# Sorting tokens by expert for two batches at a time, and sharing the copies of the transposed probabilities between two engines

## The chip, the core and the metric

The kernel runs on one core of a Trainium2 chip. The metric is the device time of one execution in microseconds (us). A core has five engines that run side by side, each through its own queue of instructions in order: TensorE (PE), VectorE (DVE), ScalarE (ACT), GpSimd (POOL) and SyncE (SP, which here only starts transfers). They wait for each other through semaphores.

## What is computed

```python
x = L0_attn_x                                   # (16, 512, 256), float32
xn = _layernorm(x, axis=-1)
x = x + attn(xn, wqkv, wo, q_norm_w, k_norm_w) + ffn(xn, gate_w, expert_w)

def attn(x, ...):                               # 16 heads of 64
    q, k, v = split(einsum('btc,oc->bto', x, wqkv))
    q = _rope(_rmsnorm(q, q_norm_w), cos, sin)  # k alike
    attn = softmax(causal(einsum('bhtd,bhsd->bhts', q, k) * 64 ** -0.5))
    return einsum('btc,oc->bto', einsum('bhts,bhsd->bhtd', attn, v), wo)

def ffn(x, gate_w, expert_w):                   # 8 experts of 256 x 256
    onehot = one_hot(argmax(einsum('bsh,eh->bse', x, gate_w), -1), 8)
    expert_out = einsum('bsh,efh->bsef', x, expert_w)
    return x + einsum('bsef,bse->bsf', expert_out, onehot)
```

Each token uses one of eight experts, the one with the highest gate score. The choice is known only while the kernel runs.

## The kernel before

The work is cut into 128 units: 16 batches of 512 tokens times 8 pairs of heads. A batch has NT = 4 row tiles of 128 tokens. Float32 products are made of three products of rounded halves (TERMS), over two chunks of the 256 inputs (NC = 2), so a 128-token tile times one weight block is six matmuls.

Each engine's program is written out by hand as a function unit(u), called for u = -1 to 130. In unit u, PE does the attention of unit u, the q, k and v products of unit u+1, and the values (L494) of unit u-1. All engines follow one pattern of four score blocks k = 0 to 3, of 256, 512, 384 and 128 columns per head (ITEMS, L28):

- scores(u, k) on PE (L466) writes ps_s, which exists once, so it waits for the exponentials of the block before.
- row_max(u, k) on DVE (L631) reads ps_s, softmax(u, k) on ACT (L342) writes prob.
- transpose_probs(u, k) on PE (L483) writes ps_p, which exists once too, and take_pt(u, k) on ACT (L350) copies both heads of it to prob_t.

Between the blocks, PE makes q, k and v of the next unit in four tiles (qkv, L431); ACT squares and copies them (take_qkv, L324); DVE multiplies by the rotation tables (rope_products, L612); POOL rotates and scales (L278, L286). At the end of the unit PE transposes the result (transpose_qk, L458), ACT takes the rounded halves k_t and q_t and DVE the remainders (take_qk, L337 and L625). Only then can scores(u+1, 0) start. The output of unit u-1 is normalised by DVE (normalise_o, L642) with the reciprocals that PE transposed (L506) and ACT copied (take_inverse, L356), is split by ACT and DVE (take_o, L363 and L647), and project(u) on PE (L449) adds it through take_projection (L662).

The experts are dense: in each unit PE multiplies all four row tiles of the batch by one expert, the one with the pair's number (experts, L440), 24 matmuls in two halves, one before the fourth score block and one after transpose_qk. DVE multiplies each result by the token's onehot column and adds it to acc (take_experts, L652). Some pairs of a batch carry more on DVE: pair 0 choose (L599), pair 4 row_stats (L569), pair 5 normalise_x (L580), pair 6 the transposed xn of the next batch (take_xt, L587), pair 7 start_rows (L593). Three PSUM banks ps_g0 to ps_g2 serve all other products in turn; g_bank (L189) works out whose turn it is, and bank (L409) waits until the use three turns back has been read:

```python
            def bank(i, *released):
                for sem, n in until[i]:
                    pe.wait_ge(sem, n)
                until[i] = released
                return ps_g[i]
```

Before the first unit the weights are loaded in seven chunks, four of w_qkv, two of w_exp and one of w_out, and DVE splits each into halves (L722 to L726).

## Time and profile before

| | us |
|---|---|
| median of three runs (lowest, highest) | 2467.36 (2464.22, 2468.24) |
| the profiled execution, its own time | 2465.25 |
| its span, first to last instruction | 2463.1 |
| busy in the span: PE / DVE / ACT / POOL | 2352.5 / 1755.1 / 1450.9 / 1172.1 |

The granted clock of PE is 0.997 of full speed as a mean over the span. A group of instructions (in the list by line) gives the busy time and the mean time of one; instructions overlap a little, so the start-to-start distance in the timeline is shorter than the duration. In the timeline a bracket at the end of a row says how long the engine was idle before it and what released it. "PEld" is PE's weight load, which runs beside its matmuls.

### The profile page before, as it was taken

To read this page: it belongs to the slowest core of one execution; us is meant where nothing else is said; L and a number is where in the kernel's file an instruction comes from. 1 tells how busy PE (TensorE), PEld (TensorE's weight loads), DVE (VectorE), ACT (ScalarE), POOL (GpSimd) and SP (SyncE) were. 2 spreads that over 40 slices of the span, in tenths; PEclk is the share of its full clock that TensorE was granted. 3 is DMA by queue.
4 is the path that set the end of the run, shared out by engine and by line. 5 is a ranking of instruction groups with operands and counts; after the bars stand their busy time and mean duration, and the time that the engine had idled before them with its cause. 6 is when DMAs were issued, how large, how long until landed. Compare 5 with 4: busy or idle time off the path is not lost.

```text
span 2463.1 us, 49058 instructions
## 1 busy us (share of the span) xinstructions
PE 2352.5 (96%) x18048; PEld 1947.8 (79%) x18048; DVE 1755.1 (71%) x4009; ACT 1450.9 (59%) x4193; POOL 1172.1 (48%) x1822
## 2 busy tenths in 40 slices
PE   2999999999999999999999999999999999999998
PEld 1788788878888887887888888788878878888886
DVE  5677777777767777777777777767777776777775
ACT  1656566655665656665665666566556656655664
POOL 1554544455454445545544444554445445445442
PEclk9999999999999999999999999999999999999999
DMA  3000000000000000000000000000000000000000
GB/s 125 1 1 6 14 1 18 1 6 14 1 18 1 18 1 1 18 1 18 1 6 14 1 18 1 5 14 1 18 1 12 8 1 18 1 18 1 5 6 9
DMA packets 19596, 26.53 MB, mean 11 GB/s; under 512 B 1952, under 2 KB 18464, under 8 KB 18976
## 3 DMA queue, kind: packets, MB, share of 16 engines
q1 hardware_dynamic: 19360, 23.41, 3.0%
q8 instruction: 145, 2.38, 0.4%
q14 instruction: 91, 0.75, 0.1%
HBM read 15.02 MB, written 8.39 MB: 10 GB/s over the span
## 4 chain that ended last, share of the span: by engine, by line
PE 73%; DVE 16%; ACT 8%; issue 2%; DMA 1%; POOL 0%; SPq 0%; DVEq 0%
PE ps_g L419 34%; PE ps_s L476 13%; PE ps_o L502 12%; PE ps_p L491 8%; ACT prob L346 4%; PE ps_s L479 4%; DVE k_t L628 3%; DVE q_t L628 3%; DVE neg_max L634 3%; ACT k_t L340 2%; PE ps_g L510 2%; DVE o_n L645 1%; DVE ln_stat L573 1%; DVE xn L583 1%; DVE onehot L609 1%
## 5 line engine op out<-in xcount | busy, mean ns | idle before, releaser
L283 POOL TENSOR_TENSOR qk_rot<-qk_cos,qk_sin 128x128 f32<-128x128 f32 x1024 | 445.5, 456 | 1203.1 <-DVE qk_sin L620 1196.5
L346 ACT ACTIVATE prob<-ps_s,neg_max 128x256 f32<-128x256 f32 (+3 forms) x1024 | 530.8, 523 | 618.6 <-DVE neg_max L634 603.7
L419 PE MATMUL ps_g<-w_qkv,xn_t 128*128 128x384 f32 (+1 forms) x3072 | 604.3, 346 | 28.6 <-DVE xn_t L590 28.6
L419 PEld LDWEIGHTS ps_g<-w_qkv,xn_t 128*128 128x128 f32 x3072 | 529.2, 189 | 29.0 <-issue 29.0
L634 DVE TENSOR_REDUCE neg_max<-ps_s 128x2 f32<-128x512 f32 (+3 forms) x512 | 419.3, 819 | 119.9 <-PE ps_s L479 119.9
L620 DVE TENSOR_TENSOR qk_cos<-ps_g,t_cos 128x256 f32<-128x256 f32 x512 | 214.9, 420 | 352.6 <-ACT v L335 352.3
L353 ACT ACTIVATE prob_t<-ps_p 128x512 f32<-128x512 f32 (+3 forms) x512 | 361.8, 707 | 165.4 <-PE ps_p L491 165.4
L419 PE MATMUL ps_g<-w_exp,xn_t 128*128 128x256 f32 x3072 | 418.6, 285 | 19.7 <-DVE acc L658 17.7
L289 POOL TENSOR_TENSOR rms_inv<-ss,neg_half 128x8 f32<-128x8 f32 x256 | 421.6, 1647 | 0.0
L419 PEld LDWEIGHTS ps_g<-w_exp,xn_t 128*128 128x128 f32 x3072 | 381.2, 189 | 33.6 <-DVE acc L658 30.7
L476 PE MATMUL ps_s<-k_t,q_t 64*128 64x256 f32 (+3 forms) x3072 | 375.5, 349 | 28.3 <-DVE q_t L628 24.1
L491 PE MATMUL ps_p<-ident,prob 128*128 128x128 f32 x2560 | 374.4, 277 | 0.5 <-ACT prob_t L353 0.5
L476 PEld LDWEIGHTS ps_s<-k_t,q_t 64*128 64x128 f32 x3072 | 228.5, 185 | 130.3 <-issue 50.2
L294 POOL TENSOR_TENSOR qk_rot<-qk_rot,rms_inv 128x256 f32<-128x256 f32 x512 | 303.2, 613 | 20.1
L502 PE MATMUL ps_o<-prob_t,v 128*64 128x512 f32 (+3 forms) x2048 | 303.9, 439 | 0.5 <-ACT prob_t L353 0.5
L491 PEld LDWEIGHTS ps_p<-ident,prob 128*128 128x128 f32 x2560 | 273.0, 141 | 22.5 <-issue 22.4
L332 ACT ACTIVATE qk_sq<-ps_g 128x256 f32<-128x256 f32 x512 | 196.6, 384 | 132.7 <-PE ps_g L419 92.1
L502 PEld LDWEIGHTS ps_o<-prob_t,v 128*64 128x64 f32 x2048 | 135.6, 136 | 151.3 <-issue 118.9
L658 DVE SCALAR_TENSOR_TENSOR acc<-ps_g,onehot,acc 128x256 f32<-128x256 f32 x512 | 221.8, 475 | 1.2 <-PE ps_g L419 1.2
L419 PE MATMUL ps_g<-w_out,o_t 128*128 128x256 f32 x1536 | 213.8, 288 | 2.8 <-DVE o_t L649 2.8
L620 DVE TENSOR_TENSOR qk_sin<-ps_g,t_sin 128x256 f32<-128x256 f32 x512 | 212.4, 415 | 0.0
L623 DVE TENSOR_REDUCE ss<-qk_sq 128x4 f32<-128x260 f32 x512 | 212.0, 414 | 0.0
(62 smaller groups left out, 2204.9 us busy)
## 6 DMA issues: line engine op xcount, KB each, us to landing
xin<-in_x SPq DMA_DIRECT2D x16, 512.0 KB, 3.9
out<-acc SPq DMA_DIRECT2D x32, 256.0 KB, 2.1
prob_t<-in_expert_t SPq DMA_DIRECT2D x2, 1024.0 KB, 4.9
prob_t<-in_wqkv_t SPq DMA_DIRECT2D x2, 772.0 KB, 5.1
prob_t<-in_wqkv_t SPq DMA_DIRECT2D x2, 768.0 KB, 5.7
prob_t<-in_wo_t SPq DMA_DIRECT2D x1, 1024.0 KB, 4.7
t_cos<-in_rope_cos SPq DMA_DIRECT2D x1, 128.0 KB, 3.8
t_sin<-in_rope_sin SPq DMA_DIRECT2D x1, 128.0 KB, 3.9
```

The costliest lines, as they stand in the source:

```text
L283: r = pool.tensor_tensor(rot[:, :, a, :], cos[:, :, a, :], sin[:, :, 1 - a, :], ALU.add)
L289: pool.tensor_tensor(rms_inv[:, ts[0]:ts[-1] + 1, :], ss[:, ts[0]:ts[-1] + 1, :], neg_half[:, :, :], ALU.pow).then_inc(s_pool_self, 1)
L294: r = pool.tensor_tensor(rot, rot, rms_inv[:, t, :].unsqueeze(2).to_broadcast([P, 4, D]), ALU.mult)
L346: r = act.activation(prob[:, n % 2, h, 0:w], ps_s[:, h, 0:w], ACT.Exp, bias=neg_max[:, i, h:h + 1], scale=1.0, accum_out=row_sum[:, u % 2, ...
L353: act.activation(prob_t[:, :, 0:i + 1, tile(i)], ps_p[:, :, 0:w].rearrange("p h (j q) -> p h j q", q=P), ACT.Copy).then_inc(s_prob_t, 1)
L419: r = pe.matmul(ps, lhs(a, c), rhs(b, c), start=(c == parts[0] and (a, b) == TERMS[0]), stop=(c == parts[-1] and (a, b) == TERMS[-1]))
L476: pe.matmul(ps_s[:, h, 0:w], q_t[rows, a, tile(i)], k_t[rows, b, 0:w], start=(m == 0), stop=(m == 2))
L491: r = pe.transpose(ps_p[:, h, tile(j)], prob[:, n % 2, h, tile(j)], ident[:, :])
L502: r = pe.matmul(ps_o[rows, j * P:], v[:, u % 3, j, rows], prob_t[:, h, j, j * P:], start=(j == 0), stop=(j == NT - 1), skip_group_check=True)
L620: r = dve.tensor_tensor(dst[:, t % 2, :].rearrange("p (n h d) -> p n h d", n=2, h=2), src, table[:, t, :, :].unsqueeze(2).to_broadcast([P, ...
L634: dve.tensor_reduce(neg_max[:, i, :], ps_s[:, :, 0:w], AX.X, ALU.max, negate=True).then_inc(s_max, 1)
L658: dve.scalar_tensor_tensor(acc[:, b % 2, t, :], ps_g[expert_bank(u, t)][:, (t % 2) * C:(t % 2 + 1) * C], onehot[:, t, pair_of(u):pair_of(u ...
```

## The change

- Tokens of two batches (a group, 1024 tokens, GROUP = 2) are sorted by expert. Each expert's tokens are padded to whole tiles of 128; a group always has NS = 15 tiles, enough for any distribution. PE counts ranks with nine small matmuls (ranks), DVE works out each token's slot and each tile's expert in 13 dependent small operations (find_slots), and POOL writes the normalised rows to DRAM at their slots with eight indirect transfers (scatter_rows).
- From unit 11 of a group's 16 on, each unit handles one sorted tile: SP loads its 128 rows and the split weights of its expert, chosen by a register (fetch); PE transposes the rows (transpose_xs) and multiplies once (expert, six matmuls); ACT and DVE split the transposed rows (take_xs); ACT copies the result (take_ys) and SP stores it. In the last group the tiles go three to a unit, in units 123 to 127.
- In the units with 11 and 12 modulo 16 of the next group, POOL gathers the results of one batch each (gather_rows, four indirect transfers), and DVE adds them to acc one unit later (add_experts). SP stores the finished batch whole.
- w_exp is no longer kept; w_out and the expert weights are split on DVE in units 0 to 7 (split_weights), the latter stored to DRAM. Four of seven chunks stay ahead of the first unit.
- take_pt is divided: ACT copies head 0 and DVE head 1. transpose_probs and values wait for both.
- Order within a unit: values(u-1) in two halves, the second together with transpose_inverse after transpose_probs(u, 1); take_inverse on ACT after softmax(u, 2); project(u) last on PE, after transpose_qk and the xn transposes; take_projection on DVE at the start of the next unit; take_qk ahead of take_xt. xn_t exists once instead of twice, xn twice, acc four times.

```diff
+
+            return batch_of(u) // GROUP if live(u) and u % (GROUP * PAIRS) == PAIRS else None
+
+        def slots_in(u):
+            return ranks_in(u - 1)
+
+        @lru_cache(None)
+        def sorted_tiles(u):
+
+            found = []
+            for g in range(G):
+                for s in range(NS):
+                    if u == (U - 5 + s // 3 if g == G - 1 else g * GROUP * PAIRS + 11 + s):
+                        found.append(g * NS + s)
+            return tuple(found)
...
+        def back_in(u):
+
+            for b in range(B):
+                g, half = divmod(b, GROUP)
+                if u == (U + half if g == G - 1 else g * GROUP * PAIRS + 27 + half):
+                    return b
+            return None
...
+        def added_in(u):
+
+            if u == U + 3:
+                return B - 1
+            b = back_in(u - 1)
+            return None if b == B - 1 else b
...
-            for c in range(NC):
-                yield (w_exp[:, :, c, :, :].rearrange("p a e n -> p a (e n)"),
-                       expert_t[:, c, :, :].rearrange("p e n -> p (e n)"))
-            yield (w_out[:, :, :, :].rearrange("p a h n -> p a (h n)"), wo_t.rearrange("p h n -> p (h n)"))
...
+            sp.dma_start(wo_raw, wo_t).then_inc(s_wo_loaded, 16)
+            sp.wait_ge(s_x_zero, 1)
+            for n in range(2):
+                sp.dma_start(x_dram[n].rearrange("(s p) c -> p s c", p=P),
+                             xn[:, 1, 0:1, :].to_broadcast([P, NS, C])).then_inc(s_zeroed, 16)
+            for e in range(2):
+                sp.dma_start(we_raw[:, e, :, :], expert_t[:, :, e, :]).then_inc(s_we_loaded[e], 16)
...
+            def fetch(i):
+
+                g, s = divmod(i, NS)
+                if i >= 2:
+                    sp.wait_ge(s_xs_t, i - 1)
+                    sp.wait_ge(s_expert, i - 1)
+                sp.wait_ge(s_scattered, 16 * GT * (g + 1))
+                sp.dma_start(x_rows_s[:, i % 2, :], x_dram[g % 2][s * P:(s + 1) * P, :]).then_inc(s_xs_loaded[i % 2], 16)
+                sp.wait_ge(s_slots, g + 1)
+                for n in range(2):
+                    sp.wait_ge(s_we_stored[n], 16 * E // 2)
+                e = sp.value_load(tile_expert_i[0:1, g % 2, s:s + 1], min_val=0, max_val=E - 1)
+                sp.dma_start(w_tile[:, i % 2, :, :, :].rearrange("p a c n -> p (a c n)").bitcast(F32),
+                             w_dram[bass.ds(e, 1), :, :, :, :].rearrange("e p a c n -> p (e a c n)"))\
+                    .then_inc(s_w_tile[i % 2], 16)
+
+            def store(i):
+                g, s = divmod(i, NS)
+                sp.wait_ge(s_ys, i + 1)
+                sp.dma_start(y_dram[g % 2][s * P:(s + 1) * P, :], y_rows_s[:, i % 2, :]).then_inc(s_y_stored[i % 2], 16)
...
+                if u == E:
+                    fetch(0)
+                    fetch(1)
+                for i in sorted_tiles(u):
+                    store(i)
+                    if i + 2 < G * NS:
+                        fetch(i + 2)
+                b = added_in(u)
+                if b is not None:
+                    sp.wait_ge(s_y_added, b + 1)
+                    sp.dma_start(out_rows[b], acc[:, b % 4, :, :]).then_inc(s_out_stored[b % 2], 16)
...
+
+            def scatter_rows(g):
+                pool.wait_ge(s_slots, g + 1)
+                if g == 0:
+                    pool.wait_ge(s_zeroed, 32)
+                for t in range(GT):
+                    pool.indirect_dma_start(x_dram[g % 2], bass.IndirectOffsetOnAxis(ap=slot_i[:, g % 2, t:t + 1], axis=0),
+                                            xn[:, t // NT, t % NT, :], None).then_inc(s_scattered, 16)
...
+                for t in range(NT):
+                    at = slot_i[:, g % 2, half * NT + t:half * NT + t + 1]
+                    pool.indirect_dma_start(y_back[:, t, :], None, y_dram[g % 2],
+                                            bass.IndirectOffsetOnAxis(ap=at, axis=0)).then_inc(s_y_back, 16)
...
+                if slots_in(u) is not None:
+                    scatter_rows(slots_in(u))
+                if back_in(u) is not None:
+                    gather_rows(back_in(u))
...
-                act.activation(prob_t[:, :, 0:i + 1, tile(i)], ps_p[:, :, 0:w].rearrange("p h (j q) -> p h j q", q=P),
-                               ACT.Copy).then_inc(s_prob_t, 1)
+                act.activation(prob_t[:, 0, 0:i + 1, tile(i)], ps_p[:, 0, 0:w].rearrange("p (j q) -> p j q", q=P),
+                               ACT.Copy).then_inc(s_prob_t0, 1)
...
+                    take_xs(u, i)
+
+                if live(u):
+                    softmax(u, 2)
                 if live(u - 1):
                     take_inverse(u - 1)
-
-                if live(u):
-                    softmax(u, 2)
+                if live(u):
                     take_pt(u, 1)
                 if live(u - 1):
                     take_o(u - 1)
+                for i in tiles[0:1]:
+                    take_ys(u, i)
+                for i in tiles[2:3]:
+                    take_xs(u, i)
...
+                if live(u + 1):
+                    take_qk(u + 1)
                 if turns_x(u):
                     take_xt(batch_of(u) + 1)
-                if live(u + 1):
-                    take_qk(u + 1)
...
-            def experts(u, ts):
-
-                b = batch_of(u)
-                ps = bank(expert_bank(u, ts[0]), (s_expert_added, NT * u + ts[-1] + 1))
-                for t in ts:
-                    r = product(ps[:, (t % 2) * C:(t % 2 + 1) * C], lambda a, c: xn_t[:, b % 2, a, c, tile(t)],
-                                lambda w, c: w_exp[:, w, c, pair_of(u), :], range(NC))
-                r.then_inc(s_expert, 1)
+            def transpose_xs(u, i):
+                pe.wait_ge(s_xs_loaded[i % 2], loads(i))
+                ps = bank(g_bank(u, f"xs{i}"), (s_xs_lo, i + 1))
+                for c in range(NC):
+                    r = pe.transpose(ps[:, tile(c)], x_rows_s[:, i % 2, tile(c)], ident[:, :])
+                r.then_inc(s_xs_t, 1)
+
+            def expert(u, i):
+                pe.wait_ge(s_xs_lo, i + 1)
+                pe.wait_ge(s_w_tile[i % 2], loads(i))
+                product(bank(g_bank(u, f"ex{i}"), (s_ys, i + 1))[:, 0:C], lambda a, c: x_cols_s[:, i % 2, a, c, :],
+                        lambda w, c: w_tile[:, i % 2, w, c, :], range(NC)).then_inc(s_expert, 1)
...
+                g, n = ranks_in(u), (GT + 1) * E
+                pe.matmul(ps[:, 0:n], tri_b[:, :], onehot_b[:, :], start=True, stop=False, skip_group_check=True)
+                for back in range(1, GT + 1):
+                    r = pe.matmul(ps[:, back * E:n], ones_b[:, :], onehot_b[:, 0:n - back * E], start=False,
+                                  stop=(back == GT), skip_group_check=True)
+                r.then_inc(s_rank, 1)
...
-                group, half, i = projection(u)
+                group, half = projection(u)
                 pe.wait_ge(s_o_lo, 2 * group + 2)
-                ps = bank(i, (s_proj_added, u - 2))
+                pe.wait_ge(s_wo_split, pair_of(2 * group) + 2)
+                ps = bank(g_bank(u, "proj"), (s_proj_added, u - 2))
...
-                    values(u - 1)
+                    values(u - 1, (0, 1))
...
+                if live(u - 1):
+                    values(u - 1, (2, 3))
+                    transpose_inverse(u - 1)
+                for i in tiles[0:1]:
+                    expert(u, i)
...
+                if live(u + 1):
+                    transpose_qk(u + 1)
...
                 if projection(u):
                     project(u)
-                if live(u):
-                    experts(u, (0, 1))
-
...
-                    transpose_qk(u + 1)
-                if live(u):
-                    experts(u, (2, 3))
...
+                dve.wait_ge(s_rank_taken, g + 1)
+                own(dve.tensor_tensor(filled[:, :, :], rank[:, GT, :].unsqueeze(2).to_broadcast([P, E, GT]),
+                                      thresholds[:, :].unsqueeze(1).to_broadcast([P, E, GT]), ALU.is_gt))
+                own(dve.tensor_reduce(tiles_of_e[:, :], filled[:, :, :], AX.X, ALU.add))
...
+                own(dve.tensor_reduce(slot[:, :], slot_of_e[:, :, :], AX.X, ALU.add))
+                dve.tensor_copy(slot_i[:, g % 2, :], slot[:, :]).then_inc(s_slots, 1)
...
+            def add_experts(b):
+                dve.wait_ge(s_y_back, 16 * NT * (b + 1))
+                dve.wait_ge(s_proj_added, PAIRS * (b + 1))
+                dve.tensor_tensor(acc[:, b % 4, :, :], acc[:, b % 4, :, :], y_back[:, :, :], ALU.add).then_inc(s_y_added, 1)
...
+            def take_pt(u, k):
+                i, w = ITEMS[k], width(k)
+                dve.wait_ge(s_pt, NT * u + k + 1)
+                dve.tensor_copy(prob_t[:, 1, 0:i + 1, tile(i)], ps_p[:, 1, 0:w].rearrange("p (j q) -> p j q", q=P))\
+                    .then_inc(s_prob_t1, 1)
...
-                    take_experts(u - 1, (2, 3))
+                    take_pt(u - 1, 3)
+                if projection(u - 1):
+                    take_projection(u - 1)
+                if live(u - 1):
                     invert_sums(u - 1)
...
                     row_max(u, 1)
+                    take_pt(u, 0)
...
-                if projection(u):
-                    take_projection(u)
                 if live(u - 1):
                     normalise_o(u - 1)
+                if live(u):
+                    take_pt(u, 1)
...
+                if slots_in(u) is not None:
+                    find_slots(slots_in(u))
...
+                if live(u):
+                    take_pt(u, 2)
...
+                if 0 <= u < E:
+                    split_weights(u)
+                if added_in(u) is not None:
+                    add_experts(added_in(u))
```

The two places that follow are from the second half of a unit.

PE, before, from the first half of the dense expert matmuls to the transposes of k; ps_s holds scores, ps_p transposed probabilities, ps_g the three shared banks:

```order
L419 MATMUL ps_g<-w_exp,xn_t 128x256 [waits s_products]
L419 MATMUL ps_g<-w_exp,xn_t 128x256 x11
L476 MATMUL ps_s<-k_t,q_t 128x128 [waits s_prob]
L476 MATMUL ps_s<-k_t,q_t 128x128 x5
L479 MATMUL ps_s<-mask_b,ident_b 128x128 x2
L491 MATMUL ps_p<-ident,prob 128x128 [waits s_prob_t,s_prob]
L491 MATMUL ps_p<-ident,prob 128x128 x5
L463 MATMUL ps_g<-ident,qk_rot 128x128 [waits s_inv_t,s_scaled]
```

The same place after the change, in a unit that has no sorted tile:

```order
L731 MATMUL ps_o<-prob_t,v 64x256 x2
L731 MATMUL ps_o<-prob_t,v 64x128 x2
L740 MATMUL ps_g<-ident,row_inv 128x128 [waits s_products,s_inv]
L740 MATMUL ps_g<-ident,row_inv 128x128 x3
L702 MATMUL ps_s<-k_t,q_t 128x128 [waits s_prob]
L702 MATMUL ps_s<-k_t,q_t 128x128 x5
L705 MATMUL ps_s<-mask_b,ident_b 128x128 x2
L718 MATMUL ps_p<-ident,prob 128x128 [waits s_prob_t1,s_prob_t0,s_prob]
L718 MATMUL ps_p<-ident,prob 128x128 x5
L689 MATMUL ps_g<-ident,qk_rot 128x128 [waits s_products,s_scaled]
```

The dense expert matmuls are gone, the second half of the values and the transposed reciprocals stand in their place, and the transposes of the probabilities wait for two copies instead of one.

DVE, before, from the third row maximum to the fourth and on to the remainders of k_t and q_t:

```order
L634 TENSOR_REDUCE neg_max<-ps_s 128x2 [waits s_scores]
L667 TENSOR_TENSOR acc<-ps_g,acc 128x512 [waits s_proj]
L645 TENSOR_TENSOR o_n<-ps_o,inv_t 128x512 [waits s_o,s_inv_t]
L634 TENSOR_REDUCE neg_max<-ps_s 128x2 [waits s_scores]
L658 SCALAR_TENSOR_TENSOR acc<-ps_g,onehot,acc 128x256 [waits s_proj_added,s_expert]
L658 SCALAR_TENSOR_TENSOR acc<-ps_g,onehot,acc 128x256
L628 TENSOR_TENSOR k_t<-ps_g,k_t 128x512 [waits s_qk_hi]
L628 TENSOR_TENSOR q_t<-ps_g,q_t 128x512 [waits s_qk_hi]
L649 TENSOR_TENSOR o_t<-o_n,o_t 128x512 [waits s_o_hi]
```

And after, in a unit with one sorted tile:

```order
L889 TENSOR_TENSOR x_cols_s<-ps_g,x_cols_s 128x256 [waits s_xs_hi]
L934 TENSOR_REDUCE neg_max<-ps_s 128x2 [waits s_scores]
L951 TENSOR_TENSOR o_n<-ps_o,inv_t 128x512 [waits s_o,s_inv_t]
L939 COPY prob_t<-ps_p 128x4x128 [waits s_pt]
L934 TENSOR_REDUCE neg_max<-ps_s 128x2 [waits s_scores]
L928 TENSOR_TENSOR k_t<-ps_g,k_t 128x512 [waits s_qk_hi]
L928 TENSOR_TENSOR q_t<-ps_g,q_t 128x512 [waits s_qk_hi]
L939 COPY prob_t<-ps_p 128x3x128 [waits s_pt]
L955 TENSOR_TENSOR o_t<-o_n,o_t 128x512 [waits s_o_hi]
L934 TENSOR_REDUCE neg_max<-ps_s 128x2 [waits s_scores]
```

The projection and the expert additions left this stretch; two copies of transposed probabilities and one split of sorted rows came in, and o_n now stands directly ahead of a copy that PE waits for.

## Rows read from the trace of the kernel before

**Rows 1.** The page, part 1: engine, busy us, share, instructions.
```profile
PE 2352.5 (96%) x18048; PEld 1947.8 (79%) x18048; DVE 1755.1 (71%) x4009; ACT 1450.9 (59%) x4193; POOL 1172.1 (48%) x1822
```

**Rows 2.** Timeline of one unit: start us, us, engine, line, operation, [idle before].
```profile
1144.20 0.69 DVE L634 TENSOR_REDUCE neg_max<-ps_s 128x2 f32<-128x512 f32 x1 [0.33 <-PE ps_s L479]
...
1149.40 1.21 DVE L634 TENSOR_REDUCE neg_max<-ps_s 128x2 f32<-128x1024 f32 x1
...
1153.21 0.42 DVE L620 TENSOR_TENSOR qk_cos<-ps_g,t_cos 128x256 f32<-128x256 f32 x1 [2.59 <-ACT v L335]
...
1154.21 0.95 DVE L634 TENSOR_REDUCE neg_max<-ps_s 128x2 f32<-128x768 f32 x1
...
1155.19 0.58 ACT L346 ACTIVATE prob<-ps_s,neg_max 128x384 f32<-128x384 f32 x1 [1.52 <-DVE neg_max L634]
...
1156.12 1.58 PE L419 MATMUL ps_g<-w_exp,xn_t 128*128 128x256 f32 x12
...
1157.63 0.55 PE L476 MATMUL ps_s<-k_t,q_t 64*128 64x128 f32 x6
...
1158.44 0.42 DVE L634 TENSOR_REDUCE neg_max<-ps_s 128x2 f32<-128x256 f32 x1 [0.83 <-PE ps_s L479]
...
1158.90 1.04 PE L463 MATMUL ps_g<-ident,qk_rot 128*128 128x128 f32 x8
...
1159.60 0.59 ACT L340 ACTIVATE k_t<-ps_g 128x512 fp32r<-128x512 f32 x1
...
1160.83 0.68 DVE L628 TENSOR_TENSOR q_t<-ps_g,q_t 128x512 fp32r<-128x512 f32 x1
...
1161.56 0.62 PE L476 MATMUL ps_s<-k_t,q_t 64*128 64x256 f32 x6 [0.17 <-DVE q_t L628]
...
1162.44 0.69 DVE L634 TENSOR_REDUCE neg_max<-ps_s 128x2 f32<-128x512 f32 x1 [0.33 <-PE ps_s L479]
```

**Rows 3.** List by shape: line, engine, operation, tiles, count | busy, mean ns.
```profile
L628 DVE TENSOR_TENSOR k_t<-ps_g,k_t 128x512 fp32r<-128x512 f32 x128 | 88.4, 690 | 75.8 <-ACT k_t L340 75.8
...
L725 DVE CAST w_qkv<-prob_t 128x1544 fp32r<-128x1544 f32 x2 | 1.9, 960 | 1.7 <-DMA prob_t<-in_wqkv_t 1.7
...
L289 POOL TENSOR_TENSOR rms_inv<-ss,neg_half 128x8 f32<-128x8 f32 x256 | 421.6, 1647 | 0.0
```

**Rows 4.** Timeline of POOL: the same rotation of two batches.
```profile
1110.03 1.79 POOL L283 TENSOR_TENSOR qk_rot<-qk_cos,qk_sin 128x128 f32<-128x128 f32 x4 [7.03 <-DVE qk_sin L620]
...
1259.85 1.79 POOL L283 TENSOR_TENSOR qk_rot<-qk_cos,qk_sin 128x128 f32<-128x128 f32 x4 [7.04 <-DVE qk_sin L620]
```

**Rows 5.** Timeline of DVE: what one unit of a batch adds to its stream.
```profile
1117.79 0.36 DVE L602 MAX8 top<-scores_g 128x8 f32<-128x8 f32 x4
...
1120.55 0.69 DVE L667 TENSOR_TENSOR acc<-ps_g,acc 128x512 f32<-128x512 f32 x1
...
1194.02 1.40 DVE L573 BATCH_NORM_STATS2 ln_stat<-xin 128x6 f32<-128x256 f32 x4
...
1195.94 0.42 DVE L634 TENSOR_REDUCE neg_max<-ps_s 128x2 f32<-128x256 f32 x1
...
1213.27 1.38 DVE L583 TENSOR_SCALAR xn<-xin,ln_mv,ln_rstd 128x256 f32<-128x256 f32 x4
...
1240.38 1.22 DVE L597 TENSOR_TENSOR acc<-xin,xn 128x1024 f32<-128x1024 f32 x1
```

**Rows 6.** Timeline of DVE at the start: fourth weight chunk and last weight chunk.
```profile
24.12 1.76 DVE L726 TENSOR_TENSOR w_qkv<-prob_t,w_qkv 128x1536 fp32r<-128x1536 f32 x1
...
37.72 2.29 DVE L726 TENSOR_TENSOR w_out<-prob_t,w_out 128x2048 fp32r<-128x2048 f32 x1
```

**Rows 7.** DMA issues: out<-in, queue, kind, count, KB, median us to landing.
```profile
xin<-in_x SPq DMA_DIRECT2D x16, 512.0 KB, 3.9
...
out<-acc SPq DMA_DIRECT2D x32, 256.0 KB, 2.1
```

**Rows 8.** Timeline of PE: first score block of the last unit.
```profile
2433.31 0.62 PE L476 MATMUL ps_s<-k_t,q_t 64*128 64x256 f32 x6 [0.17 <-DVE q_t L628]
```

312 lines of the change are left out of this document (238 added, 74 removed).

## The prediction

> **What bounds the kernel now.** I read the page's busy times first. PE is busy 96% of the span, DVE 71% [rows 1], so PE seems to be the bound and the removal of matmuls seems to be worth its full time. The timeline of one plain unit says how far that goes [rows 2]. Count from the first row maximum of a unit, 1144.20, to the next, 1162.44: the period is 18.24 us. Times below, in us, count from that first row maximum. The reader should follow DVE and ACT, not PE: second row maximum at 5.20, rotation products of tile 3 at 9.01, third row maximum at 10.01, its exponentials at 10.99. Then DVE waits for PE: scores 3 begin at 13.43, once the dense expert half (1156.12, 1.51 us to the next row) is through, and the fourth maximum begins at 14.24. From there it is a chain again: transposes of k and q on PE at 14.70, ACT's k_t at 15.40, DVE's q_t from 16.63 to 17.31, scores of the next unit at 17.36, with a 0.17 us wait for q_t ahead of them. So two nearly equal limits stand side by side: PE's stream, and one serial chain through DVE and ACT. Every engine's queue is in order and ps_s and ps_p exist once, so a shorter PE stream doesn't let the next block start early.
>
> A whole batch takes 149.82 us [rows 4], 3.9 more than 8 x 18.24 = 145.9. These are the extra steps of some pairs [rows 5], which now hide partly in the time in which DVE waits for PE.
>
> **PE's side of the change.** Removed are 24 matmuls per unit, 2 x 1.51 = 3.0 us [rows 2], 387 us in all. Added are 120 tiles of six matmuls (0.75) and two transposes (0.2), about 0.9 per unit. PE's stream falls from 18.1 to 16.0 us. Alone that would be worth some 270 us.
>
> **A plain unit after the change**, walked through with the same rows:
> - Up to 5.20 nothing moves: DVE's fourth copy of prob_t and the projection's addition replace two expert additions of the same length.
> - ACT's first copy of prob_t is halved, so the products of tile 3 start at 8.64 instead of 9.01. But the split of the sorted rows (256 columns, as a rotation product 0.34) now stands ahead of the third maximum: 9.98 instead of 10.01. Its exponentials end about 12.2.
> - take_inverse now stands behind these exponentials: a 512-column copy on ACT, 0.59 as k_t [rows 2], from 12.09 to 12.69. Only then normalise_o (0.68 long, 0.60 to the next start) from 12.72, then DVE's 512-column copy of prob_t.
> - For that copy no row exists. The bounds are the conversion from SBUF (0.96 us for 1544 columns, 0.32 for 512) and the subtraction that reads PSUM, 0.69 [rows 3]. I take 0.69, since the source is PSUM. It ends at 14.01. PE's third transposes wait for it and run 14.05 to 14.71, where transpose_qk starts: before, it was 14.70.
> - The fourth maximum starts at 13.93, 0.31 earlier, but k_t is now held by the transposes, about 15.37; q_t ends at 17.3 and scores of the next unit start at 17.35. DVE then still has 384 columns of prob_t (0.5) and take_o (0.6), and reaches the next first maximum at 18.3.
>
> So the unit takes 18.25 us as before; the bound moved to DVE and ACT and 2 us of PE become waiting. With the shorter copy it would be 18.0, with each new DVE step 0.05 longer 18.4. Over 127 units that is -30 to +20, and I take 0. The Trainium skill, "VectorE: DVE Perf Modes", The perf-mode tier table, states that float32 copies run at double rate only from SBUF and at single rate with a PSUM operand. By that rule the copy is at the PSUM end; without it, at SBUF rate, the sum below would be 30 us lower. No run here shows such a copy yet.
>
> **Extras of each batch.** With DVE on the chain they count nearly in full [rows 5]. Statistics: 1194.02 to 1195.94, 1.92, less 0.3 of slack: 1.6. Normalise: 1.3 less 0.3: 1.0. Choose: 1117.79 to 1120.55, 2.76 plus a small copy, against 1.85 that DVE would wait for the inverse: 1.0. start_rows: 1.22 long, 0.9 net. Pair 6: the second bank for xn is that of kt and the projection's that of qt, so project waits for q_t and its 1.5 us follow it: 1.45. Sum 6.0 against 3.9: +2.1, times 15 batches, +32.
>
> **Extras of each group.** find_slots is 13 dependent operations ahead of the fourth maximum. The nine small ones of the statistics take 0.21 each and a 256-column one 0.42 [rows 5], so 2.6 to 5.5; I take 3.2, less slack, 2.9. In the rank unit project waits for k_t's bank: 0.9. add_experts, 1.2 as start_rows, at the end of two units: 2.3. One unit of 16 has no tile: -0.3. POOL: the eight scatters start when the slots are known, 17.2 into the unit, and the next rotation is due at 24.2 with 0.3 of slack. No row shows what one holds POOL for. The bounds are its plain addition (1.79 us for four, 0.45 each, in [rows 4]) and its power operation, 1.65 [rows 3]. I take 1.0, half way, since neither is nearer: 0.7 late; at 0.45 nothing, at 1.65 6 us. Behind the waiting rotation stand DVE's products, the chain itself. The second gather waits for add_experts of the first batch, at 19.5, and costs 0.7 in the same way (0 to 3.3). The sum is 7.2 per group, 50 for seven, and 4 for the last group's slots: +54 (+42 to +115).
>
> **SP.** Its queue blocks at the fetch of the next group's first tile, as in unit 24, until that group is scattered in units 25 and 26. Behind it stand one store, which ACT first needs two tiles later in unit 28, and the next fetch, for unit 28 too; the load of xin has gone out in unit 23. I cost it at nothing: an ordinary tile has a whole unit, 18 us, between fetch and use, against 3.9 us for 512 KB [rows 7]. If that cover were gone, PE would stand at transpose_xs by the lateness itself.
>
> **Ends.** Start: w_exp and w_out go from the front; DVE ended chunk four at 25.88 and chunk seven at 40.01 [rows 6]: -14. Units 0 to 7: splits of 256 and 512 columns at 0.62 and 1.15 ns per column [rows 3, 6] with gaps 1.5 us each at the end of the unit, 12, less 0.34 for 11 units without tiles: +8. Units 123 to 127 have three tiles and two buffers: the third tile's rows can be fetched only after the first tile's result is copied, 14.4 into the unit. Rows of 256 KB land in 2.1 and 512 KB in 3.9 [rows 7], so PE stands at transpose_xs until about 17.3, with scores 3 behind it, and then the rest of the chain follows: 5.9 per unit, four units before the last score block, +24 (10 to 40). Tail: from the first scores of the last unit, 2433.31 [rows 8], to the end is 29.8 now. After: last expert result at 18.7, store 2.5, gather 4.0 + 2.1, addition 1.3, the second gather 6.1 and addition 1.3, store 3.9, and the small rest: 41, so +11. Each of these gathers is 128 KB. The Trainium skill, "DMA: Bandwidth & Descriptors", Anatomy of one DMA, gives about 2.0 us plus bytes over 436 GB/s for such a transfer; by that estimate it is 2.3, near the 2.1 of the row, and if POOL were held for all of it the eight scatters would be a rival, below.
>
> **Sum:** 0 + 32 + 54 - 14 + 8 + 24 + 11 = +115, on the profiled execution's 2465.25: 2580. The median stands 2 above it: 2582 us. A difference of 0.2%, 5 us, is about what a measurement can tell from no change.
>
> **Rivals.**
> - *PE's time comes through* (faster). If the chain of DVE and ACT had over 1 us of slack that my walk doesn't see, PE would set the pace: 16.0 plus 0.3 of waits, 1.9 less per unit, -240, with the other terms halved by PE's cover +60: about 2290. It decides once q_t ends before 16.3 instead of 17.3. For it: PE's 96%. Against it: DVE and ACT rows up to 10.99 have no PE wait of size in them. Chance 9%.
> - *The chain shortens a little*: the cheap copy, cheap indirect transfers and hidden extras. -30, -12, and half of the 32, with 10 less at the end: about 2510. For it: both low bounds are measured rows. Chance 15%.
> - *POOL is held long by indirect transfers.* At 1.65 and above the rotations come 6 and 3 us late in each group, and at 2.3 each, 11 and 6: +60 to +110, about 2660. For it: POOL writes 128 addresses each. Chance 20%.
> - *The forecast*: 55%.
>
> The range goes from 2520 to 2655: it takes in the unknown copy, the small operations and the indirect transfers up to 1.65, most of the second and third rival, and leaves out the first. Faster is the first rival and a last 1% of the second, 10%. No change would need the extras to vanish, 1%. Slower has the rest, 89%.
>
> **What would show it.** A plain unit of 18.2 us with PE idle 2 us in it, ahead of scores 3 and the third transposes; the copy from ps_p at 0.69 for 512 columns; the fourth maximum directly behind it; pair 4 near 19.9; stalls at transpose_xs in units 123 to 127; first matmul near 27.5; tail of 40. I am wrong if plain units are under 17.5, if indirect transfers cost POOL other than 1 us, or if PE waits for tiles in ordinary units.

## The result and the profile after

The changed kernel takes 2716.86 us (2715.13 to 2719.62) against 2467.09 before: ratio 1.1015, 95% interval 1.0996 to 1.1034. It is slower, as forecast, but by 250 us instead of 115, outside the range. The profiled execution has a span of 2713.6 us.

The page of the profile of the changed kernel, rows from parts 1, 2 and 4 (compare [rows 1]):

```profile
PE 2292.2 (84%) x16008; PEld 1797.7 (66%) x16008; DVE 1843.4 (68%) x4300; ACT 1387.6 (51%) x4433; POOL 1299.7 (48%) x1957
...
PEclk8999999989999999999999999998999989999988
...
DVE 45%; ACT 18%; PE 18%; issue 12%; POOL 7%; DMA 1%; SPq 0%; POOLq 0%; ACTq 0%; DVEq 0%
```

PE issues 2040 matmuls fewer, yet is busy for only 60 us less. A plain unit at full clock has PE busy for 16.78 us against 18.07 before, which over 127 units would be 164 less. The clock row says where the rest went: the mean granted clock is 0.943 of full, 0.997 before, and a plain unit with the low clock in it has PE busy for 18.23. The chain of waits ran over PE for 73% of the span before, now for 18%, and over DVE for 45%.

The timeline of one plain unit with a tile, columns as in [rows 2]:

```profile
1373.89 0.69 DVE L934 TENSOR_REDUCE neg_max<-ps_s 128x2 f32<-128x512 f32 x1 [0.78 <-PE ps_s L705]
...
1382.54 0.42 DVE L920 TENSOR_TENSOR qk_cos<-ps_g,t_cos 128x256 f32<-128x256 f32 x1 [1.48 <-POOL qk_rot L446]
...
1383.87 0.95 DVE L934 TENSOR_REDUCE neg_max<-ps_s 128x2 f32<-128x768 f32 x1
...
1385.98 0.59 ACT L547 ACTIVATE inv_t<-ps_g 128x512 f32<-128x512 f32 x1
...
1386.61 0.69 DVE L951 TENSOR_TENSOR o_n<-ps_o,inv_t 128x512 f32<-128x512 f32 x1 [1.79 <-ACT inv_t L547]
...
1387.22 0.68 DVE L939 COPY prob_t<-ps_p 128x512 f32<-128x512 f32 x1
...
1387.81 0.41 DVE L934 TENSOR_REDUCE neg_max<-ps_s 128x2 f32<-128x256 f32 x1
...
1388.04 0.85 PE L718 MATMUL ps_p<-ident,prob 128*128 128x128 f32 x6 [1.14 <-DVE prob_t L939]
...
1388.73 1.04 PE L689 MATMUL ps_g<-ident,qk_rot 128*128 128x128 f32 x8
...
1389.36 0.60 ACT L526 ACTIVATE k_t<-ps_g 128x512 fp32r<-128x512 f32 x1 [0.29 <-PE ps_g L689]
...
1389.52 1.67 PE L629 MATMUL ps_g<-w_out,o_t 128*128 128x256 f32 x12
...
1390.60 0.68 DVE L928 TENSOR_TENSOR q_t<-ps_g,q_t 128x512 fp32r<-128x512 f32 x1
...
1392.27 0.68 DVE L934 TENSOR_REDUCE neg_max<-ps_s 128x2 f32<-128x512 f32 x1
```

This is the walk of the prediction almost to the tenth: inverse at 12.09 from the first maximum (forecast 12.09), normalisation at 12.72 (12.72), DVE's copy at 13.33, fourth maximum at 13.92 (13.93), k_t at 15.47 (15.37), period 18.38 (forecast 18.25). PE waits for 0.32 us ahead of scores 3 and for 1.14 ahead of the third transposes. But look at the same place one unit later, on PE alone:

```profile
1406.42 1.11 PE L718 MATMUL ps_p<-ident,prob 128*128 128x128 f32 x6 [1.13 <-DVE prob_t L939]
1407.32 1.91 PE L689 MATMUL ps_g<-ident,qk_rot 128*128 128x128 f32 x8
1408.88 2.28 PE L629 MATMUL ps_g<-w_out,o_t 128*128 128x256 f32 x12
```

The wait is the same, 1.13 us, but the eight transposes of q and k take 1.91 instead of 1.04. The stretches of this unit show the granted clock (columns: stretch, its us, PE busy and instructions, clock, DMA share, GB/s):

```profile
1406.00:1406.50 0.50, 0.08 (x1) 1.00 0.00 0
1406.50:1407.00 0.50, 0.50 (x5) 0.86 0.00 0
1407.00:1407.50 0.50, 0.50 (x4) 0.50 0.05 16
...
1410.50:1411.00 0.50, 0.50 (x6) 1.00 1.00 410
```

Half a microsecond behind the idle time the clock falls from 2.4 to 1.2 GHz, and it is full again at 1410.5. In between stands the chain's own piece, the transposes that k_t and q_t come from, and the next unit starts 1.3 us late. By whole units, from one first maximum to the next, columns as before:

```profile
1046.05:1064.49 18.44, 16.80 (x127) 1.00 0.12 38
1064.49:1084.21 19.72, 18.25 (x127) 0.91 0.14 47
1084.21:1102.59 18.38, 16.78 (x127) 1.00 0.11 37
1102.59:1122.49 19.90, 16.74 (x127) 1.00 0.14 47
1122.49:1142.19 19.70, 18.22 (x127) 0.91 0.13 41
```

Of 127 units 72 have a clock below 0.985; before it was one, the very first. Of the plain units (pairs 1 to 3 of a group, from unit 17 on) it is 11 of 21, and in all 11 the clock falls within 1.1 us of the end of the wait; the wait is 1.13 or 1.14 in the other ten too. Of the units of pair 0, where the choice of the expert makes the wait 2.05 us (1365 to 1368, and 385 to 387), it is 13 of 14 from unit 16 on. The Trainium skill, "TensorE: Matmul & The Clock Gate", HAM oscillation, describes this mechanism, PE throttled behind idle time, but for far longer pauses than these; by that rule these waits would cost nothing, and the rows above say otherwise.

The length of a wait doesn't decide alone. The unit of 19.90 us above, a pair 4, has the same wait of 1.14 and a second of 1.69 in front of the next scores, and keeps its full clock, as all seven of its kind do:

```profile
1116.75 0.85 PE L718 MATMUL ps_p<-ident,prob 128*128 128x128 f32 x6 [1.14 <-DVE prob_t L939]
...
1121.57 0.62 PE L702 MATMUL ps_s<-k_t,q_t 64*128 64x256 f32 x6 [1.69 <-DVE q_t L928]
```

Nor does every low unit cost time: from unit 25 on, up to the last tiles, the units 9 of a group take 20.97 to 21.00 us and the units 12 take 21.03 to 21.05, whether their mean clock is below 0.985 or not.

Where the 250 us lie (start is up to the first row maximum of unit 0, the tail runs from that of unit 127 to the end of the span):

| stretch | before | after | difference | forecast |
|---|---|---|---|---|
| start | 60.5 | 46.5 | -14.0 | -14 |
| units 0 to 7 | 147.6 | 166.5 | +18.9 | +10 |
| units 8 to 122 | 2153.1 | 2346.3 | +193.2 | +84 |
| units 123 to 126 | 73.0 | 110.4 | +37.4 | +24 |
| tail, with unit 127 | 28.9 | 43.9 | +15.0 | +11 |

POOL's timeline in the unit of the scatters:

```profile
1221.30 1.09 POOL L465 DMA_INDIRECT x_dram<-xn,slot_i  x1 [4.08 <-DVE slot_i L885]
1222.69 0.97 POOL L465 DMA_INDIRECT x_dram<-xn,slot_i  x1 [0.30 <-issue]
...
1230.31 0.96 POOL L465 DMA_INDIRECT x_dram<-xn,slot_i  x1 [0.30 <-issue]
1231.28 1.70 POOL L446 TENSOR_TENSOR qk_rot<-qk_cos,qk_sin 128x128 f32<-128x128 f32 x4
```

Each transfer is 0.96 long, near the 1.0 that I took, but 1.27 from start to start: eight are 10.0 us. The rotation was due about 3.1 after the first maximum of 1224.97, at 1228.1, and came 3.2 late, where the prediction had 0.7.

### The profile page after: what moved, and what is told of

Its sections match the earlier page's. It is cut to its first block, busy times and chain, and to the rows that moved or that the text cites. A ratio compares the mean times of both kernels' runs of the same rounds, so it can differ in the third digit from the quotient of the medians.

```text
span 2713.6 us, 47127 instructions
## 1 busy us (share of the span) xinstructions
PE 2292.2 (84%) x16008; PEld 1797.7 (66%) x16008; DVE 1843.4 (68%) x4300; ACT 1387.6 (51%) x4433; POOL 1299.7 (48%) x1957
## 4 chain that ended last, share of the span: by engine, by line
DVE 45%; ACT 18%; PE 18%; issue 12%; POOL 7%; DMA 1%; SPq 0%; POOLq 0%; ACTq 0%; DVEq 0%
DVE neg_max L934 11%; ACT prob L532 9%; DVE qk_sin L920 5%; PE ps_g L629 5%; DVE qk_cos L920 5%; PE ps_p L718 4%; DVE prob_t L939 4%; DVE ss L923 4%; PE ps_g L689 3%; DVE o_n L951 3%; POOL qk_rot L446 2%; ACT inv_t L547 2%; ACT qk_sq L518 2%; DVE k_t L928 2%; PE ps_s L702 2%
## 5 line engine op out<-in xcount | busy, mean ns | idle before, releaser
L629 PE MATMUL ps_g<-w_qkv,xn_t 128*128 128x384 f32 (+1 forms) x3072 | 618.3, 349 | 25.1 <-DVE xn_t L835 14.9
L629 PEld LDWEIGHTS ps_g<-w_qkv,xn_t 128*128 128x128 f32 x3072 | 535.7, 191 | 32.9 <-DVE acc L966 17.6
L718 PE MATMUL ps_p<-ident,prob 128*128 128x128 f32 x2560 | 399.7, 290 | 153.1 <-DVE prob_t L939 153.1
L718 PEld LDWEIGHTS ps_p<-ident,prob 128*128 128x128 f32 x2560 | 288.8, 147 | 247.5 <-issue 246.3
L539 ACT ACTIVATE prob_t<-ps_p 128x256 f32<-128x256 f32 (+3 forms) x512 | 225.1, 440 | 232.8 <-PE ps_p L718 223.0
L731 PE MATMUL ps_o<-prob_t,v 128*64 128x512 f32 (+3 forms) x2048 | 341.1, 456 | 0.4 <-ACT prob_t L539 0.4
L939 DVE COPY prob_t<-ps_p 128x256 f32<-128x256 f32 (+3 forms) x512 | 247.2, 483 | 27.8 <-PE ps_p L718 27.8
L928 DVE TENSOR_TENSOR k_t<-ps_g,k_t 128x512 fp32r<-128x512 f32 x128 | 88.6, 692 | 243.8 <-ACT k_t L526 239.7
L629 PE MATMUL ps_g<-w_out,o_t 128*128 128x256 f32 x1536 | 242.3, 313 | 5.4 <-DVE k_t L928 3.3
L951 DVE TENSOR_TENSOR o_n<-ps_o,inv_t 128x512 f32<-128x512 f32 x128 | 88.5, 691 | 219.5 <-ACT inv_t L547 219.2
L629 PEld LDWEIGHTS ps_g<-w_out,o_t 128*128 128x128 f32 x1536 | 221.0, 218 | 9.0 <-issue 7.4
```

What stands on the lines that cost most here:

```text
L629: r = pe.matmul(ps, lhs(a, c), rhs(b, c), start=(c == parts[0] and (a, b) == TERMS[0]), stop=(c == parts[-1] and (a, b) == TERMS[-1]))
L718: r = pe.transpose(ps_p[:, h, tile(j)], prob[:, n % 2, h, tile(j)], ident[:, :])
L731: r = pe.matmul(ps_o[rows, j * P:], v[:, u % 3, j, rows], prob_t[:, h, j, j * P:], start=(j == 0), stop=(j == NT - 1), skip_group_check=True)
L939: dve.tensor_copy(prob_t[:, 1, 0:i + 1, tile(i)], ps_p[:, 1, 0:w].rearrange("p (j q) -> p j q", q=P))\
```

## Experiments

There are twelve kernels; "low units" are those of the 127 with a mean granted clock below 0.985. All times are medians of four or more runs, with the kernel before at 2466 to 2468 beside them.

| run | us | low units | units 8 to 122 |
|---|---|---|---|
| before | 2467 | 1 | 2153 |
| changed kernel | 2717 | 72 | 2346 |
| a1_fill | 2656 | 20 | 2281 |
| a2_pt_early | 2482 | 37 | 2131 |
| a3_gather_late | 2686 | 74 | 2319 |
| a4_scatter_split | 2681 | 69 | 2313 |
| a5_no_split | 2620 | 26 | 2255 |
| a6_inverse_early | 2570 | 34 | 2206 |
| a7_order_before | 2569 | 46 | 2204 |
| b1_thin | 2471 | 53 | 2159 |
| b2_split | 2477 | 1 | 2162 |
| c1_combined | 2408 | 9 | 2055 |
| c2_ends | 2393 | 11 | 2057 |
| c3_no_split | 2401 | 2 | 2067 |

**a1_fill: give PE something to do in the wait.**

```diff
+            def keep_busy(u, n):
...
+                for _ in range(n):
+                    pe.matmul(ps_g[i][:, 0:3 * PW], xn_t[:, 0, 0, 0:P], w_qkv[:, 0, 0, E:E + 3 * PW], start=True, stop=True)
...
                     scores(u, 3)
+                    if live(u + 1):
+                        keep_busy(u, 5 + (4 if pair_of(u) in (CHOOSE_PAIR, STATS_PAIR, NORM_PAIR) else 0))
                     transpose_probs(u, 2)
```

> The changed kernel plus matmuls whose result nobody reads, put where PE now waits for the second head's copy of prob_t: 5 of 384 columns (about 1.1 us) between scores 3 and the third transposes in every unit, 9 in the pairs 0, 4 and 5. Nothing else moves. Theory C (the clock): behind its idle time PE's granted clock falls to half in 72 of 127 units, and what then runs at half speed stands on the chain. If so, PE has more to do and the kernel is faster: plain units at 18.4 us instead of 18.4 and 19.7, clock near 1.00 in the units with the fill, about 70 units x 1.3 us = 90 less, some 2630 us (2620 to 2660). Rival W (the waits of DVE and ACT alone set 19.7, the low clock only goes with them): no unit gets shorter, 2717 to 2735.

Measured 2656.41 us (2650.72 to 2659.3). More work, 60 us faster, though less than the 90 that I had expected. PE's waits for prob_t in the changed kernel and in this one, columns: engine, tile, line <- what it waited for: us, times, longest:

```profile
PE ps_p L718 <- DVE prob_t L939: 153.1, 123, 2.4
```

```profile
PE ps_p L725 <- DVE prob_t L948: 22.6, 92, 0.8
```

and its plain units by stretches:

```profile
1026.55:1044.96 18.41, 17.66 (x132) 1.00 0.13 47
1044.96:1063.32 18.36, 17.68 (x132) 1.00 0.14 44
1063.32:1081.69 18.37, 17.68 (x132) 1.00 0.13 44
```

The pace of DVE and ACT has stayed at 18.4; only the 19.7s are gone. So the low clock is a cause of its own and not a companion of the waits: theory C holds, rival W falls. The fill takes 66 us out of units 8 to 122 (2346 to 2281), and 20 low units remain, so the low clock costs at least that. Much of it is not in plain units. Unit 58, in which the rotations come late behind the scatters (the timeline of POOL above), in the changed kernel and with the fill:

```profile
1224.97:1249.37 24.40, 18.35 (x119) 0.86 0.28 93
```

```profile
1201.42:1222.54 21.12, 18.28 (x124) 0.92 0.32 107
```

Its first rotation starts 6.3 us after the first maximum in both. The eight units of this kind are 19 us shorter together with the fill.

**b1_thin: take PE's work away and nothing else**, in the kernel before. It leaves out the correction terms of the experts' product.

```diff
-                    r = product(ps[:, (t % 2) * C:(t % 2 + 1) * C], lambda a, c: xn_t[:, b % 2, a, c, tile(t)],
-                                lambda w, c: w_exp[:, w, c, pair_of(u), :], range(NC))
+                    for c in range(NC):
+                        r = pe.matmul(ps[:, (t % 2) * C:(t % 2 + 1) * C], xn_t[:, b % 2, 0, c, tile(t)],
+                                      w_exp[:, 0, c, pair_of(u), :], start=(c == 0), stop=(c == NC - 1))
```

> The kernel before with the dense experts' product cut to one of its three terms: 8 matmuls of 256 columns per unit instead of 24, 2.0 us of PE less per unit, which is what the change takes away net (it leaves out the correction terms of the experts' product). Nothing else changes. If PE were the bound: 2467 - 250 = 2215. My step (the chain of DVE and ACT stands beside PE at 18.2 us): plain units 18.0 to 18.25, 2435 to 2467. Theory C on top of it: the idle time lowers the clock in part of the units, which then take 19 to 19.6: 2470 to 2550, slower with less work.

Measured 2470.58 us (ratio 1.0014, interval 1.0004 to 1.0024): 2 us of matmuls less per unit, some 256 in all, and no gain. Its units by stretches, pairs 1, 2, 3 and, further on, 6 and 7:

```profile
980.91:999.42 18.51, 17.32 (x127) 0.94 0.04 15
999.42:1016.95 17.53, 16.33 (x127) 1.00 0.14 46
1016.95:1034.46 17.51, 16.32 (x127) 1.00 0.00 1
...
1222.03:1242.62 20.59, 19.21 (x134) 0.91 0.00 1
1242.62:1261.75 19.13, 17.89 (x127) 0.92 0.00 1
```

Two things stand in it. Plain units at full clock fall to 17.51 from 18.25: the chain of the old order had 0.7 us of slack that my reading of [rows 2] did not see. And 53 units have a low clock, so that pair 1 takes 18.5 to 18.9 instead of 17.5, pair 6 20.2 to 20.6 against 19.9 before, and pair 7 up to 19.1 against 18.3, and it is all given back. PE waits for 1.12 to 1.16 us in every unit of pairs 2 and 3 as well, and none of the 14 from unit 18 on has a low clock.

**a5_no_split: undo the split in the changed kernel.**

```diff
-                act.activation(prob_t[:, 0, 0:i + 1, tile(i)], ps_p[:, 0, 0:w].rearrange("p (j q) -> p j q", q=P),
+                act.activation(prob_t[:, :, 0:i + 1, tile(i)], ps_p[:, :, 0:w].rearrange("p h (j q) -> p h j q", q=P),
                                ACT.Copy).then_inc(s_prob_t0, 1)
...
-                    pe.wait_ge(s_prob_t1, n)
...
-                dve.tensor_copy(prob_t[:, 1, 0:i + 1, tile(i)], ps_p[:, 1, 0:w].rearrange("p (j q) -> p j q", q=P))\
-                    .then_inc(s_prob_t1, 1)
+                return
```

> The changed kernel with the split of the probabilities' copy undone: ACT copies both heads in one instruction, as before the change, at its place in the changed order; DVE copies nothing. Theory S: the split itself is small. ACT's copy of the second prob_t (1024 columns, about 1.1 us behind the inverse) frees the third transposes at about the same time as DVE's copy behind the normalisation, but it pushes o_t and the fourth exponentials by 0.3, and products 3 come 0.4 later again: 0.3 to 0.6 us more per unit, 2740 to 2790. Rival D: DVE's copies are themselves what lengthens the chain; then it is faster without them, 2640 to 2700.

Measured 2619.58 us (2618.45 to 2624.97), 97 faster; I had expected it slower. The timeline at the third transposes, in a unit whose first maximum is at 1326.20:

```profile
1338.99 1.03 ACT L539 ACTIVATE prob_t<-ps_p 128x1024 f32<-128x1024 f32 x1
...
1340.17 0.85 PE L717 MATMUL ps_p<-ident,prob 128*128 128x128 f32 x6 [0.72 <-ACT prob_t L539]
```

ACT's one copy of 1.03 us starts right behind the inverse, and PE's third transposes begin 13.97 after the first maximum, 0.2 earlier than behind DVE's copy in the changed kernel. A plain unit is 18.13, 0.25 less. More than that, the wait is 0.72 now, half of the difference because scores 3 come 0.2 later, and in plain units the clock did not fall: 26 low units instead of 72. I had also overrated what the longer copies cost ACT: the rotation products of tile 3 come 0.2 later, not 0.4.

**b2_split: the split alone in the kernel before.** Edit: the same two copies, DVE's directly behind the row maxima.

> The kernel before with the split alone: ACT copies head 0, DVE head 1, DVE's copies directly behind the row maxima; dense experts and the order of the work stay. Theory: PE's 18.1 us per unit bound a plain unit here, so the split shows only in the units with extra steps: 2445 to 2468. Rival: the 2.0 us more on DVE per unit lengthen its chain by 0.2 or more, 2485 or more.

Measured 2476.65 us (2475.45 to 2479.51), 11 more than before: neither range. Plain units are 18.25 as before; pair 0 has 19.44 instead of 19.04 and pair 7 18.55 instead of 18.27, which over 16 batches is the difference.

**a6_inverse_early: the old order around the inverse back, the split kept.**

```diff
-                if live(u):
-                    softmax(u, 2)
                 if live(u - 1):
                     take_inverse(u - 1)
+                if live(u):
+                    softmax(u, 2)
...
-                    values(u - 1, (0, 1))
+                    values(u - 1, (0, 1, 2, 3))
...
+                if live(u - 1):
+                    transpose_inverse(u - 1)
...
                     transpose_probs(u, 1)
-                if live(u - 1):
-                    values(u - 1, (2, 3))
-                    transpose_inverse(u - 1)
```

> The changed kernel with the order around the inverse put back as before the change: values undivided behind scores 1, the inverse transposed ahead of scores 2 and copied by ACT ahead of the third exponentials. The split copies and the sorted experts stay. Theory O (the order is what put the normalisation and DVE's second copy behind the exponentials): o_n no longer waits for the inverse, the third transposes follow scores 3 directly, plain units 17.6 to 18.1 instead of 18.4, and with less idle time in one piece fewer units at the low clock: 2550 to 2640. Rival: values in one piece delay products 3 and the third maximum by as much as is won, 2690 to 2720.

Measured 2570.02 us (2567.75 to 2571.3), 147 faster. Plain units are 17.47, a little better than the 17.6 to 18.1 expected. This order, which put inverse, normalisation and second copy in a row behind the exponentials, is the largest single part.

**a7_order_before: the old order around the inverse and no split.** Edit: both of the above. What is left of the change is the sorting, and with it what neither edit puts back: project(u) as the last of PE, take_projection in the next unit, take_qk ahead of take_xt, xn_t once.

> The same, and the split undone too: ACT copies both heads. What is left of the change is the sorted experts (tiles, ranks, slots, scatter, gather, late loading of expert weights). Theory: split and order together cost some 150 to 200 of the 250 us, the sorting the rest; a plain unit is that of the kernel before with fewer matmuls, 17.5 as in the thinned kernel, pairs 8 to 13 with their scatters and gathers stay long: 2530 to 2590. Rival: undoing the split adds nothing to undoing the order, within 10 us of the run before.

Measured 2569.43 us (2566.64 to 2572.59). The range was met, but the rival is right about the split: in the old order it is worth nothing in the sum. Unit by unit it isn't nothing: plain units are 17.80 without it and 17.47 with it (I had expected 17.5), pair 0 is 19.07 instead of 20.9, and gains and losses cancel. So the 250 us are 147 for the order around the inverse and what the split and the clock make of it, and 102 for the sorting and the smaller moves, which no run tells apart. Of these 102 units 123 to 126 with the tail hold 55 (113.4 + 43.8 against 73.0 + 28.9).

**a3_gather_late and a4_scatter_split: POOL's queue.**

```diff
-                if u == (U + half if g == G - 1 else g * GROUP * PAIRS + 27 + half):
+                if u == (U + half if g == G - 1 else g * GROUP * PAIRS + 27 + 2 * half):
```

> The changed kernel with the second gather of each group, and its addition, one unit later, so that POOL no longer waits in front of its rotations for the addition of the first half. Theory P (POOL's queue): pair 13 of a group falls from 23.65 us to 20.5 to 21, seven groups x 3 = 20 less, 2690 to 2700. Rival G (what costs there is the four gathers' own 5 us on POOL, wherever they stand): 2712 to 2720, the 3 us move to the next unit.

Measured 2685.8 us (2679.54 to 2693.12), 31 less, a little more than expected. Unit 13 of a group fell from 23.65 to 19.7, since POOL no longer stands in front of its rotations waiting for the addition.

```diff
-                    scatter_rows(slots_in(u))
+                    g = slots_in(u)
+                    scatter_rows(g, range(GT if g == G - 1 else NT))
+                if slots_in(u - 1) is not None and slots_in(u - 1) < G - 1:
+                    scatter_rows(slots_in(u - 1), range(NT, GT))
```

> The changed kernel with the eight scatters of a group issued by POOL as four behind unit 16g+9 and four behind unit 16g+10, instead of eight in a row (the last group keeps them together). Eight take 10 us, start to start 1.26 each, from 17.2 us into the unit, so that the next unit's rotations come some 3 us late. Theory P (POOL's queue): pair 10 of a group falls from 24.3 us to 20.5 to 21, seven groups x 3.5 = 25 less, 2685 to 2700. Rival: the 5 us of the second four reach the next rotation as well, 2712 to 2720.

Measured 2680.95 us (2675.82 to 2692.95), 36 less; unit 58, number 10 of its group, fell from 24.4 to 19.4. The same transfers, at other places in POOL's queue: theory P holds for both. But the 36 us are not POOL's alone: the fill took 3.3 of the 5.0 us out of unit 58 with the scatters where they were, so lateness and low clock share this price, and the runs don't part them further.

**a2_pt_early: a third order.** PE does values 2 and 3 ahead of the second transposes, so that prob_t is free earlier; DVE copies before the fourth maximum, and the normalisation comes last.

```diff
                     softmax(u, 2)
+                if live(u):
+                    take_pt(u, 1)
                 if live(u - 1):
                     take_inverse(u - 1)
-                if live(u):
-                    take_pt(u, 1)
-                if live(u - 1):
-                    take_o(u - 1)
...
                     take_xt(batch_of(u) + 1)
+                if live(u - 1):
+                    take_o(u - 1)
...
                     scores(u, 2)
+                if live(u - 1):
+                    values(u - 1, (2, 3))
+                if live(u):
                     transpose_probs(u, 1)
                 if live(u - 1):
-                    values(u - 1, (2, 3))
                     transpose_inverse(u - 1)
...
-                if live(u - 1):
-                    normalise_o(u - 1)
                 if live(u):
                     take_pt(u, 1)
...
                     row_max(u, 3)
+                if live(u - 1):
+                    normalise_o(u - 1)
```

The first two pieces are ACT's program, the third PE's, the last two DVE's.

> The changed kernel in another order: PE multiplies values 2 and 3 ahead of the second transposes; DVE copies its head of the second prob_t ahead of the unit before's normalisation instead of behind it, and takes the fourth maximum first; ACT copies its head ahead of the inverse and takes o_t after q_t. The same work. Theory Q (the place of the copy behind the inverse and the normalisation is on the chain, my step of the plain unit): the third transposes no longer wait for prob_t, k_t comes 0.6 to 0.7 us earlier, plain units 17.7 instead of 18.4: 127 x 0.65 = 80 less, and with theory C less idle time in front of PE, thus fewer units at the low clock, up to 60 less again: 2580 to 2640. Rival: the chain runs elsewhere (rotation products and exponentials), then 2700 to 2717.

Measured 2482.36 us (2478.15 to 2483.51), 234 less, far more than expected. Its timeline around the same place:

```profile
978.40 0.69 DVE L936 TENSOR_REDUCE neg_max<-ps_s 128x2 f32<-128x512 f32 x1
...
989.25 0.68 DVE L941 COPY prob_t<-ps_p 128x512 f32<-128x512 f32 x1
...
990.50 0.59 ACT L539 ACTIVATE prob_t<-ps_p 128x512 f32<-128x512 f32 x1
...
990.98 0.60 ACT L547 ACTIVATE inv_t<-ps_g 128x512 f32<-128x512 f32 x1
...
991.26 0.82 PE L718 MATMUL ps_p<-ident,prob 128*128 128x128 f32 x6
...
991.46 0.43 DVE L936 TENSOR_REDUCE neg_max<-ps_s 128x2 f32<-128x256 f32 x1 [1.53 <-PE ps_s L705]
...
991.80 0.68 DVE L953 TENSOR_TENSOR o_n<-ps_o,inv_t 128x512 f32<-128x512 f32 x1
```

DVE's copy now runs in time in which it had nothing else, and the third transposes follow scores 3 without a wait, 12.86 after the first maximum and so 1.29 earlier than in the changed kernel. That is the whole of what a plain unit gains: it is 17.12 us, 1.26 less, with PE busy for 16.56 of them. I had expected 0.65. Which of the three moves brings how much was not tried. The 37 low units that remain are among those with extra steps.

**c1_combined and c2_ends: a version that beats both.** c1 is a2, a3 and a4 together, the choice of the expert behind DVE's copy (its one-hot rows later still), and both additions of 1024 columns on POOL.

> A version meant to beat both: the order of the early copies (2482), the second gather a unit later, the scatters four and four, the choice of the expert behind DVE's copy of prob_t and its one-hot rows for the first batch of a group a unit later, and the two additions of 1024 columns per batch (start of the rows, gathered expert rows) on POOL instead of DVE. From the units of the early order: gather 3.3 x 7 = 23 less, scatters 2.5 x 7 = 17, choice 1.5 x 16 = 24, the additions 1.0 x 32 = 32: 2385 (2370 to 2420). Rival: POOL's additions, about 2.4 us each by its 256-column product of 0.61, or PE idle elsewhere give part of it back: 2420 to 2460.

Measured 2407.68 us (2402.15 to 2408.83), inside the range, with 9 low units left. POOL's addition takes 2.37 us for DVE's 1.22, and POOL has the time. c2 changes the end too (and splits the scatters of the last group and gathers its results a unit later):

```diff
-                    if u == (U - 5 + s // 3 if g == G - 1 else g * GROUP * PAIRS + 11 + s):
+                    if u == ((U - 5 + s // 2 if s < 10 else U + (s - 10) // 3) if g == G - 1 else g * GROUP * PAIRS + 11 + s):
```

> The combined version with another end: of the last 15 tiles two stand in each of the units 123 to 127 and five behind the last unit, instead of three in each of 123 to 127, so that every tile's rows can be loaded a unit ahead; the last group's scatters are split four and four as well. Theory: units 123 to 126 fall from 25.5 us to 18 to 19, 28 less, unit 122 from 21.1 to 18.2, 3 less, and the tail grows by 10 to 16: 2387 to 2398. Rival: the tiles in the tail cost as much as is won there, 2400 to 2415.

Measured 2393.22 us (2390.62 to 2394.51), ratio to before 0.9698, interval 0.9681 to 0.9714. Units 123 to 126 fall from 102.0 to 73.6, the tail grows from 43.0 to 61.3, 18 us where I had allowed 10 to 16. What stood there in the changed kernel is PE waiting for the third tile's rows, as forecast:

```profile
2576.87 0.69 PE L654 MATMUL ps_g<-ident,x_rows_s 128*128 128x128 f32 x2 [5.41 <-DMA x_rows_s<-x_dram]
2577.22 1.63 PE L629 MATMUL ps_g<-w_tile,x_cols_s 128*128 128x256 f32 x6
2578.77 0.90 PE L702 MATMUL ps_s<-k_t,q_t 64*128 64x128 f32 x6
```

Behind the 5.41 us of idle time the expert's six matmuls take 1.63 instead of 0.95 (at 1384.87 in the plain unit), and the scores 0.90 instead of 0.55: the low clock again.

**c3_no_split: the split undone in that version.**

> The combined version with its ends mended (2393), the split undone: ACT copies both heads in one instruction, DVE none. In this order ACT's copy of the second prob_t stands between the third exponentials and the inverse, and ACT then works without a pause up to q_t. Theory: one instruction of 1024 columns for one of 512 puts 0.45 us on ACT's chain there, plain units 17.4 to 17.6 instead of 17.1, 2425 to 2450: here the split is worth its copies, other than in the changed kernel. Rival: PE's own 16.6 us and DVE's relief of 2 us per unit make up for it, 2385 to 2400.

Measured 2400.73 us (2398.56 to 2403.04), 7.5 slower than with the split. That is far from the 2425 to 2450 of the theory and next to the rival's range. The expected lengthening is there (plain units 17.64 instead of 17.11), but most of the units 9, 11 and 13 of a group are shorter in return, by 0.4 to 0.9, about 2 and up to 1.9, and only 2 low units are left. The same edit is worth -97, 0, -11 and +7.5 us in four kernels: the changed one, the one with the old order around the inverse, the kernel before, and c2_ends (minus: the kernel is faster without the split).

## Why the prediction was wrong, step by step

- **The plain unit at 18.25, "the bound moved to DVE and ACT and 2 us of PE become waiting".** As a walk of waits it was right: 18.38 at full clock, copy 0.68 for 0.69. The Trainium skill, "VectorE: DVE Perf Modes", The perf-mode tier table, states the single rate for a float32 copy with a PSUM operand, and the trace agrees with the same 0.68 us for 512 columns. The 0.13 us more are some 16 us over the kernel, inside the -30 to +20 that I gave this term. The step that failed is the price of the waiting: I costed it at nothing. In front of a wait of 1.14 us stands full clock, behind it in about half of the plain units 1.2 GHz, and what runs there is on the chain. The fill shows 66 us for it between units 8 and 122, about half of the 135 us by which the sum was short; in the long units it did not remove the low clock, so there it may be more.
- **PE's stream at 16.0.** Mis-sized: at full clock PE is busy for 16.78, so the waiting is 1.6 us and not 2. In front of a pause a group of matmuls counts with its whole length (the six of the expert take 0.95, not the 0.75 of the sum), and the values now come in two pieces. It cost nothing by itself, since PE is not the bound in a plain unit.
- **The two limits side by side.** I took the old chain for as long as PE's stream. b1_thin says 17.5, not 18.25. That is why I saw no room for an order that is better or worse, and did not ask what the new order costs: a6_inverse_early prices the order around the inverse at 147 with the clock's part, and a2_pt_early shows that another order of the same instructions has 17.1.
- **Extras of a batch.** At full clock right: pair 4 19.90 for 19.85, pair 5 19.27 for 19.25, pair 0 19.28 (in a1_fill) for 19.25, pair 7 19.33 for 19.15, pair 6 20.0 for 19.7. Pair 0 has a wait of 2.05 us and with it the low clock: 20.6.
- **Extras of a group: the scatters 0.7 late, the second gather 0.7.** Mis-sized. find_slots took 2.99 (3.2 forecast), but an indirect transfer costs POOL 1.27 from start to start and not 1.0, and the lateness is what is left over the slack, so a quarter more made it 3.2. The runs price the two places at 36 and 31 us where the sum had 5 each. With the fill, units 10 of a group are 21.1 and units 13 are 23.6, where my terms make 18.95 and 21.15: some 17 and 15 us of lateness over the kernel. The rest of the 36 is in good part the clock; what the rest of the 31 is, the runs don't show. The rival with POOL held long had the right mechanism. That the 67 us fall into its 60 to 110 is luck: POOL was held for 1.27, not 1.65 or more.
- **SP costs nothing.** Right: PE waited for x_rows_s five times in the whole kernel, 25.4 us, all of it from unit 123 on.
- **Ends.** Start right to 0.1. Units 0 to 7 +18.9 for +10, low clock in six of them. Units 123 to 126 +37.4 for +24 by the forecast mechanism; the low clock behind each stall was not in it. Tail +15.0 for +11.
- **The sum.** Of the 135 us missing, 66 are the clock by the fill, about 44 are left in units 8 to 122 with the fill (2281 less 2153 less the forecast 84: the late rotations and the 0.12 per unit make 46 by my reckoning), and 26 are in the ends.
- **The rival on the other side (PE's time comes through)** was rightly given little for this order. b1_thin shows why it is hard here: shortening PE alone leaves idle time in long units and takes the gain back.

Still open is how much of the 147 us of the order is chain and how much is clock: a1_fill removes most low units but not those behind waits elsewhere. Nor was it tried to fill the waits of the early order. What besides the length of a wait makes the clock fall is open too.

## What to carry to other kernels

When a change takes work off the fullest engine and leaves the chain, the time that engine now waits is not free: on PE ask how long each new wait is and what stands behind it, since the matmuls there may run at 1.2 GHz. Price a copy or a split only together with its place in each engine's queue; the same split was worth anything from a loss of 97 us to a gain of 7.5. A price taken from one run holds for the clock of that run too: moving the scatters looked like 36 us of POOL's time and was in good part PE's clock. And where an engine issues several indirect transfers in a row, spread them over the units in which it idles.

## What was not expected of the hardware

- Waits of 1.14 us on PE in an 18.4 us unit were followed by the low clock in 11 of 21 plain units and not in the others, waits of 2.05 us in 13 of 14 units of pair 0, waits of 0.72 us in none of the 21 plain units of a5_no_split. But waits of 1.12 to 1.16 us were followed by it in none of the 14 units of pairs 2 and 3 of b1_thin, and 1.14 with 1.69 behind it in none of the seven units of pair 4 of a group. What tells them apart the runs don't show.
- Matmuls whose results nobody reads made the kernel 60 us faster.
- An indirect transfer of 128 rows of 1 KB holds POOL for 0.96 us and is followed by 0.30 without work, scatter (L465) and gather alike.
- Additions of 128x1024 float32 from SBUF take 2.37 us on POOL, 1.22 on DVE.
